# The down weights of an expert read in place instead of from a copy, in the two expert layers of a macaron block

## The reference

```python
x = x + 0.5 * moe(layernorm(x))
x = x + mamba1(layernorm(x)) + flip-side mamba2(layernorm(x))
x = x + 0.5 * moe(layernorm(x))

# moe: E = 8 experts, hidden width I = 512, each token goes to its best K = 2
logits = x_flat @ gate_w.T
top_v, top_i = top_k(logits, 2); probs = softmax(top_v)
for e in experts:
    hidden = silu(x_flat @ wg[e].T) * (x_flat @ wu[e].T)
    out += combine[e][:, None] * (hidden @ wd[e].T)
```

## Time and profile before

| | us |
|---|---|
| median of 3 runs | 2813.0 |
| lowest, highest | 2808.58, 2814.91 |
| span of the profiled execution | 2637.8 |
| routing and loading ahead of the first tile loop | 0 to 104 |
| tile loop of `moe(0)`, first fetch to last store issued | 104 to 496 |
| Mamba stage and routing of `moe(1)` | 496 to 2203 |
| tile loop of `moe(1)` | 2203 to 2594 |
| combining and storing the result | 2594 to 2637.8 |

### The profile page before, as it was taken

The page is one execution under the profiler, slowest core; times in us unless marked ns, Lnnn a source line. Parts: engine busy times, 40 slices in busy tenths (PEclk is TensorE's granted clock), DMA queues, the critical chain, the costliest instruction groups (busy, mean ns, idle before and its releaser), DMA issues.

```text
span 2637.8 us, 49017 instructions
## 1 busy us (share of the span) xinstructions
PE 2244.2 (85%) x15840; PEld 1920.7 (73%) x15840; DVE 2254.8 (85%) x3430; ACT 1909.6 (72%) x3628; POOL 2198.0 (83%) x1402
## 2 busy tenths in 40 slices
PE   4899999768888898898898898988988768999992
PEld 3799999547676677777777676766777647999982
DVE  8766666789999999999999999999999897666666
ACT  4355555378998998998999899999898544555551
POOL 3577777369999999999999999999999936777771
PEclk8899999889999999999999999999999878999996
DMA  7011111433333333333333333333333240111116
GB/s 247 17 48 50 49 49 49 121 107 104 105 109 106 109 102 101 106 107 100 109 103 102 110 103 105 110 106 106 105 102 111 76 160 25 49 50 49 49 50 204
DMA packets 156813, 248.60 MB, mean 94 GB/s; under 512 B 22082, under 2 KB 66018, under 8 KB 155874
## 3 DMA queue, kind: packets, MB, share of 16 engines
q1 hardware_dynamic: 137568, 202.79, 25.9%
q0 software_dynamic: 18208, 37.26, 5.2%
q10 hardware_dynamic: 866, 6.43, 0.6%
HBM read 213.10 MB, written 33.29 MB: 93 GB/s over the span
## 4 chain that ended last, share of the span: by engine, by line
POOL 28%; PE 23%; issue 22%; DVE 14%; ACT 8%; DMA 4%; POOLq 0%; ACTq 0%; DVEq 0%; SPq 0%
POOL buf L484 10%; POOL buf L545 9%; DVE buf L914 6%; PE bank L1544 6%; POOL token_outputs L494 5%; PE bank L1419 4%; DMA buf<-state_rows 3%; PE bank L1329 3%; PE bank L1519 3%; POOL buf L532 2%; DVE buf L901 2%; ACT scaled L1194 2%; ACT over L1161 2%; DVE bank L886 2%; PE bank L1348 2%
## 5 line engine op out<-in xcount | busy, mean ns | idle before, releaser
L545 POOL TENSOR_TENSOR buf<-buf 128x1024 f32<-128x1024 f32 x512 | 1199.9, 2378 | 33.8 <-PE bank L1544 28.9
L914 DVE TENSOR_TENSOR_SCAN buf<-over,bank 128x512 f32<-128x512 f32 x832 | 953.6, 1198 | 5.2 <-PE bank L1519 2.6
L1161 ACT ACTIVATE over<-wgu,negA 128x510 f32<-128x510 f32 x832 | 541.2, 710 | 39.6 <-DVE buf L914 28.5
L1544 PE MATMUL bank<-id_sb,buf 128*128 128x128 f32 x4096 | 521.8, 282 | 6.3 <-POOL buf L545 6.3
L1544 PEld LDWEIGHTS bank<-id_sb,buf 128*128 128x128 f32 x4096 | 483.9, 146 | 55.8 <-issue 46.5
L1348 PE MATMUL bank<-parts 128*128 128x256 f32 x3408 | 480.3, 291 | 3.3 <-DVE buf L764 1.9
L1348 PEld LDWEIGHTS bank<-parts 128*128 128x128 f32 x3408 | 428.8, 192 | 7.2 <-issue 4.1
L1194 ACT ACTIVATE scaled<-wd_sb,I 128x256 f32<-128x256 f32 x896 | 377.3, 498 | 22.3 <-PE bank L1519 22.2
L494 POOL DMA_INDIRECT token_outputs<-buf,slot_out x284 | 287.7, 1013 | 111.1 <-issue 83.2
L484 POOL DMA_INDIRECT buf<-token_rows,slot_token x284 | 297.1, 1046 | 95.4 <-issue 89.7
L1519 PE MATMUL bank<-id_sb,scaled 128*128 128x128 f32 x1792 | 257.2, 281 | 91.3 <-ACT scaled L1194 40.8
(11 more groups left out here) (170 smaller groups left out, 2978.0 us busy)
## 6 DMA issues: line engine op xcount, KB each, us to landing
buf<-state_rows SPq DMA_DIRECT2D x608, 256.0 KB, 3.2
token_rows<-buf SPq DMA_DIRECT2D x32, 256.0 KB, 2.3
wd_sb<-token_outputs SPq DMA_DIRECT2D x16, 512.0 KB, 4.1
buf<-token_outputs SPq DMA_DIRECT2D x16, 512.0 KB, 4.9
buf<-token_rows,slot_token POOLq DMA_INDIRECT x284, 2.6
token_outputs<-buf,slot_out POOLq DMA_INDIRECT x284, 2.3
out<-X SPq DMA_DIRECT2D x16, 256.0 KB, 3.8
wgu<-wgT ACTq DMA_DIRECT2D x1, 2048.0 KB, 8.1
```

The source lines that it names most:

```text
L545: pool.tensor_tensor(hC[:, b, :].rearrange("p (c w) -> p c w", c=C), hs[:, b, :].rearrange("p (c w) -> p c w", c=C), Cs[:, b, :].unsqueeze ...
L914: V.tensor_tensor_scan(hs[:, b, w], dA[:, b, c, :, :].rearrange("p s t -> p (s t)"), source, 0.0, ALU.mult, ALU.add).then_inc(s[f"scan_don ...
L1161: ins = A.activation(dA[:, n % R, c, :, 1:], delta[r][:, c * W:(c + 1) * W].rearrange("p (s t) -> p s t", s=S)[:, :, 1:], ACT.Exp, scale=n ...
L1544: ins = M.matmul(bank[4 + q // 2][:, at:at + P], hC[:, n % R, c * W + q * P:c * W + (q + 1) * P], id_sb[:, :], is_transpose=True, start=Fa ...
```

## The change

DVE no longer copies the down weights of the tile's expert, and the buffer `wd_e` is gone; `wlo_dve` is raised by the second subtraction. PE loads the tile's expert number into a register itself (`expert_of(i - 1)`), ahead of `turn_slots(i + 1)`, and the eight matmuls of `down(i - 1)` read `wd_sb` at an address made from that register.

```diff
-        wd_e = carve(1040, 4 * IC * D).rearrange("p (b w) -> p b w", w=IC * D)
...
-                def low_w(i, q, e):
+                def low_w(i, b, e):
 
                     dve.wait_ge(s["whi_act"], m * TILES + i + 1)
                     wait(dve, s["up_pe"], 2 * (m * TILES + i) - 2)
                     for k, w in ((0, wg_sb), (1, wu_sb)):
-                        V.tensor_tensor(w_lo[:, q % 2, k * I:(k + 1) * I], w[:, bass.ds(e * I, I)],
-                                        w_hi[:, q % 2, k * I:(k + 1) * I].bitcast(F32), ALU.subtract)
-                    wait(dve, s["down_pe"], m * TILES + i - 3)
-                    V.tensor_copy(wd_e[:, q, :].rearrange("p (c d) -> p c d", d=D),
-                                  wd_sb[:, bass.ds(e * IC, IC), :]).then_inc(s["wlo_dve"], 1)
+                        ins = V.tensor_tensor(w_lo[:, b, k * I:(k + 1) * I], w[:, bass.ds(e * I, I)],
+                                              w_hi[:, b, k * I:(k + 1) * I].bitcast(F32), ALU.subtract)
+                    ins.then_inc(s["wlo_dve"], 1)
...
-                def down(i, b, q):
+                def expert_of(i):
+                    return pe.value_load(te[0:1, bass.ds(i, 1)], min_val=0, max_val=E - 1)
+
+                def down(i, b, e):
                     pe.wait_ge(s["hid_dve"], 2 * (m * TILES + i) + 2)
                     wait(pe, s["yo_act"], m * TILES + i)
                     for h in range(HT):
                         for c in range(IC):
                             ins = M.matmul(bank[7][:, h * D:(h + 1) * D],
                                            hid[:, b, c * TP + h * P:c * TP + (h + 1) * P],
-                                           wd_e[:, q, c * D:(c + 1) * D], start=(c == 0), stop=(c == IC - 1))
+                                           wd_sb[:, bass.ds(e * IC + c, 1), :].rearrange("p c d -> p (c d)"),
+                                           start=(c == 0), stop=(c == IC - 1))
                     ins.then_inc(s["down_pe"], 1)
 
                 def four(k, count=4):
                     for q in range(count):
                         i = k * 4 + q
+                        first = isinstance(i, int) and i == 0
+                        if not first:
+                            e = expert_of(i - 1)
                         if not (isinstance(i, int) and i == TILES - 1):
                             turn_slots(i + 1, (q + 1) % 4, k + 1 if q == 3 else k)
                         gate(i, q % 2, 0)
                         up(i, q % 2, 0)
-                        if not (isinstance(i, int) and i == 0):
-                            down(i - 1, (q - 1) % 2, (q - 1) % 4)
+                        if not first:
+                            down(i - 1, (q - 1) % 2, e)
                         gate(i, q % 2, 1)
                         up(i, q % 2, 1)
...
-                down(TILES - 1, (TILES - 1) % 2, LAST - 1)
+                down(TILES - 1, (TILES - 1) % 2, expert_of(TILES - 1))
```

More of the change, by code:

```diff
@@ L783, in four @@
                         if more:
-                            low_w(i + 1, (q + 1) % 4, e)
+                            low_w(i + 1, (q + 1) % 2, e)
                         hidden(i, q % 2, 0)
```

## The result

| | before | after |
|---|---|---|
| median, us | 2813.95 (4 runs, 2808.58 to 2816.86) | 2828.18 (4 runs, 2820.61 to 2832.42) |
| span of the profiled execution | 2637.8 | 2818.4 (time of this execution: 2820.61) |
| tile, loop one and two: first to last transposes, divided by 70 | (479.5 - 108.4)/70 = 5.30; (2577.7 - 2207.4)/70 = 5.29 | (568.4 - 108.5)/70 = 6.57; (2758.3 - 2295.4)/70 = 6.61 |

The ratio is 1.0046, with a 95% interval of 1.0033 to 1.006: the change makes the kernel slower by 0.46%. The forecast was 0.9% faster.

The account below looks back on a forecast made before the run. POOL's indirect DMAs were taken to bound the expert loops; 24.0 us from POOL plus 0.9 us at loop starts, with PE's load and addresses at nothing, gave 2813.0 - 24.9 = 2788 us, range 2780 to 2804.

Parts of the forecast that it names:

- What lies around its span (175.2 us against the median) is not touched, so the difference carries over: Whole kernel: the gain computed on the profiled span of 2637.8 us comes off the 2813.0 us median unchanged.
- after the first store POOL runs without a stop: Expert tile loops: POOL never waits for another engine between first store and last fetch; its tile takes 5.34 us.
- Copy gone, POOL's side: POOL's indirect DMAs in both expert layers: without the copy they fall to 0.987 us each, saving 24.0 us.
- My counter-example: POOL's store wholly under two subtractions (L761) took 0.98 us, cited against the subtractions stretching the DMAs.
- Rival A: POOL's DMAs stay at 1.03 us, stretched by the copy's neighbours; only 0.9 us gained, 2812 us; chance 0.06.
- Copy gone, start of each loop: First gate and first store of each expert loop come 0.42 to 0.55 us sooner; twice, 0.9 us.
- 0.5 us goes into 2.0 us: cost nothing: PE's expert-number load per tile: 0.5 us on a sequencer running 2.0 us ahead of the array, so no cost.
- nothing for the addresses: Four register steps of some 0.05 us among `down`'s first matmuls cost nothing, at most 0.2 us per PE tile.
- the cover: PE's sequencer runs 2.0 and 1.9 us ahead of its array, in stretches without a wait, hiding the load.
- Rival C: Load and addresses exposed on PE: tile 5.57 us, over POOL's 5.34; slower, 2842 us; chance 0.07.

Follow-up runs that it names:

- the first experiment: The kernel before, unchanged, with a profile of its own: 2793.1 us against 2793.8 (0.9998).
- plain DMAs: Kernel before and changed kernel, POOL's indirect fetches and stores replaced by same-size plain DMAs from SyncE, rows in order: 2571.21 and 2571.18 us (0.9207 and 0.9202).
- the paced before: Kernel before, with the fetch of tile i+5 put behind the store of tile i and waiting for tile i+1's second multiply: 2810.3 us, 0.9979.
- pace: Changed kernel, with the fetch of tile i+5 put behind the store of tile i and waiting for tile i+1's second multiply: 2840.9 us, 1.0093.

## Why the prediction was wrong

*"What lies around its span (175.2 us against the median) is not touched, so the difference carries over"*. This step failed first. The 175.2 us did not lie around the span, since a time is its span plus 2.2. No trace shows before on the chip of the result, but on that of the first experiment its span is 2789.3 - 2637.8 = 151.5 us longer than the one I read, and (6.40 - 5.30) x 140 = 154 us of tile time account for all of it. I had a profile of a chip with signals on time beside times of a chip with late ones, and took the gap for overhead. So "after the first store POOL runs without a stop" was true of the rows and not of the 2813 us: there POOL waits for `yo` (92.1 us in the first loop of the first experiment, 92.5 us in the changed kernel), and taking the copy away gave nothing (1.0014).

*"Copy gone, POOL's side"*, with its 24.0 us. This failed on its own, also where POOL is the bound: it gave 0. The 138 DMAs that overlap a copy did take 1.165 us, but every copy follows two subtractions at once, and the same 138 are exactly those that start in a subtraction. My counter-example was misread: the store at 2234.29 started 0.07 us ahead of the subtraction (2234.36) and was let through; what waits is a DMA that starts while one runs. Without the copy as many DMAs are stretched (126 against 128), and again 138 start in a subtraction, at 1.163 us. Rival A named this mechanism, the subtractions as one of two candidates, with a chance of 0.06. Its price was near: 0.9 us faster than before, where the run gave 3.0 us slower, 1.0011 (1.0001 to 1.002). The Trainium skill has the rule that I should have weighed (SBUF — State Buffer, section "Who interferes with whom"): a VectorE instruction with two SBUF inputs contends with a GpSimd instruction that reads SBUF, and the port pair that they share is an exclusive lock. `L761` has two SBUF inputs, and a DMA that starts during one ends a fixed 0.83 or 0.87 us behind its end; the trace agrees with this. The page also infers that `tensor_tensor` leaves descriptor writing alone; here it doesn't leave indirect DMAs alone, and the measurement decides.

*"Copy gone, start of each loop"*, 0.9 us. Right where signals are on time. The first gate waits for `L760`, and counted from the loop's first fetch it starts 0.63 us sooner in the first layer and 0.29 in the second (8.37 us in both, instead of 9.00 and 8.66), together 0.9. The first store came sooner by more, 1.7 and 1.6 us. In the first layer one reason is to be seen: the granted clock stood at 0.5 (its lower level, 1.2 GHz) for 10.2 us until behind the first gates, not for 13.7. From first fetch to last store the two loops took 1.9 and 2.4 us less than in the profile of before, and yet the time is no shorter; what made up for it outside the loops was not looked into.

*"0.5 us goes into 2.0 us: cost nothing"*, and nothing for the addresses. Right in size, and right where signals are on time: 302 ns for the load and 151 ns of register steps, as taken from ACT, and 0.0 us idle ahead of `down`. Two loads cost 0.02%, and with plain DMAs the whole change 0.00%. But the cover was read from a loop in which PE had no waits. Where signals are late, the load alone costs 0.21% in the kernel before and some 0.6% in the changed one. So this term, put at nothing, has most of what the change costs on the chip on which both were measured (0.6 of 0.8%).

Why it costs there is not settled. It isn't exposed ahead of the transposes (8 to 12 us idle in all these kernels), and moving it gave nothing. Nor is it shown that nothing of it is exposed ahead of `down`: there PE idles 33 to 46 us in each loop in before, with the load alone, with the fixed address and in the paced before, and 51 to 83 us in all the kernels that read `down`'s weights at an address from a register. The kernel without subtractions has fixed addresses and 65 us, so this idle time can come about in another way, and no run separates the two. What I can say is what goes with the time. The loop falls into two patterns: rows of eight DMAs, two tiles in some 13 us (6.5 each), or a row of four and a row of eight, three tiles in some 20.2 (4.9 + 6.1 + 9.2, so 6.7 each). The count of rows of up to four in both loops, without those at their starts and ends (where these are drawn moves a count by up to three), beside the ratio to before:

| kernel | rows of up to 4 | ratio |
|---|---|---|
| before | 2 | 0.9998 |
| no copy, no load, fixed address | 9 | 1.0014 |
| before with a load | 27 | 1.0021 |
| loaded once per layer | 27 | 1.0021 |
| changed, copy kept | 40 | 1.0036 |
| changed, load ahead of down | 42 | 1.0061 |
| changed, second time | 45 | 1.008 |
| changed | 62 | 1.0046 |
| before without subtractions | 62 | 1.0081 |

Adding a load on PE and taking work off DVE both move the loop towards the slower pattern. So the 0.5 to 0.8% may be not the price of an instruction but a shift in a loop whose period is set by late signals. This is argued and not shown: the rows and the ratios do not go up strictly together (45 rows with 1.008, 62 with 1.0046), and both could come from something third. Why the load costs where signals are late stays open. Rival C had the sign, with 29 us for the 14 us measured, but what it was measured against, POOL's tile of 5.34 us, did not set the time there. Whether a part of the load and the addresses is exposed on PE stays open, as said.

| place | changed kernel against before |
|---|---|
| late signals, three chips, also with pace or the load moved | 1.0046, 1.008; 1.0061, 1.0093 |
| signals on time | 1.0011 |
| plain DMAs, PE the bound | 0.9202 against 0.9207 |

## What to carry to other kernels

Before any row of a profile is used, lay its span against the timed executions: a gap much over the 2.2 us that nearly all executions here have means that the profile shows another regime than the times, and the bound read from it may not be theirs. When two instructions always follow one another, an overlap count can't tell which of them disturbs a third: sort by where the third one starts in each, or take one away. A load or copy that is hidden in a loop at one engine's full pace can still move a loop that is held by signals between engines, and taking work away can make it slower (the subtractions gone: 1.0081).

## What the runs showed of the hardware

- POOL's indirect DMAs, four per 5.3 us, make the semaphore updates of PE late on four of the six chips that the experiments met, and on that of the result, by 2 us on average after the second DMA of a row and until about 1 us behind it; ACT's and DVE's are on time. With the two fetches per 4.9 us alone it does nearly no harm. Against the profile with signals on time the tile loops are 154 of 2793 us longer, far more than the change. Not all of this is waiting: in each loop PE is busy for 376 us instead of 352, at a mean granted clock of 0.95 to 0.97 instead of 0.99 (changed kernel and first experiment, against the profile of before). On two chips it does not happen at all (before: 2639.4 and 2636.3 us). What sets the chips apart, and by which path PE's updates and these DMAs meet, stays open.
- An indirect DMA that starts during a VectorE subtraction with both inputs in SBUF, 0.2 us or more before its end, ends 0.83 (fetch) or 0.87 us (store) behind that end; one that started 0.07 us before it takes 0.98 us. Taking the subtractions away brings the mean from 1.03 to 0.99 us.
- A TENSOR_LOAD on PE takes 0.30 us, and with signals on time one per tile (in the changed kernel, 1.0011) and two (1.0002) cost next to nothing.
